# Sums of messages and of their squares: a TensorE product of the messages with themselves in place of a VectorE accumulator

## The reference, cut to what matters

```
h    = relu(layernorm(x))
node = mlp(h, W_node);  edge = mlp(edge_attr, W_edge)
msg  = relu([h[src], h[dst], edge] @ W_msg + b_msg)        # 100000 x 96
mu   = mean(msg, axis=0);  var = mean((msg - mu)**2, axis=0)
msg  = gamma * (msg - mu) * rsqrt(var + eps) + beta
out  = x + segment_sum(msg, dst) + node
```

## Time and profile before

| | us |
|---|---|
| median of 3 runs | 1090.58 (1089.98 to 1091.89) |
| profiled execution, its own time | 1093.96 |
| its span, first to last instruction | 1092.2 |
| PE busy | 839.5 (77%) |
| DVE busy | 724.6 (66%) |
| ACT busy | 542.9 (50%) |
| POOL busy | 826.6 (76%) |

### The profile page before, as it was taken

One profiled execution on the slowest core, in us unless ns is written; L12 is line 12 of the kernel. 1 busy time (PEld: TensorE's weight loads), 2 busy tenths in 40 slices (PEclk: granted clock), 3 DMA queues, 4 the chain that ended last, 5 costly groups with the idle time before them and its releaser, 6 DMA issues.

```text
span 1092.2 us, 23979 instructions
## 1 busy us (share of the span) xinstructions
PE 839.5 (77%) x6383; PEld 726.1 (66%) x6385; DVE 724.6 (66%) x1579; ACT 542.9 (50%) x1012; POOL 826.6 (76%) x786
## 2 busy tenths in 40 slices
PE   2537866639999999999777777777777776877777
PEld 2425622229999999999666666667667666766663
DVE  8678799978898898988444454444444444444445
ACT  3735988836666666666333333333333333333330
POOL 6877777777777777777777777777777777777771
PEclk9867988869999999999888888887898887888889
DMA  8665333352222222222222222222222222222223
GB/s 278 184 225 135 75 85 89 86 150 60 61 57 65 60 58 63 61 59 62 54 49 53 51 52 50 55 49 50 49 56 49 51 54 50 53 49 53 51 45 96
DMA packets 79842, 82.82 MB, mean 76 GB/s; under 512 B 52322, under 2 KB 57074, under 8 KB 79690
## 3 DMA queue, kind: packets, MB, share of 16 engines
q0 software_dynamic: 25024, 38.49, 16.6%
q1 hardware_dynamic: 54148, 42.83, 14.0%
q10 hardware_dynamic: 646, 1.25, 0.4%
HBM read 65.84 MB, written 13.34 MB: 72 GB/s over the span
## 4 chain that ended last, share of the span: by engine, by line
PE 31%; POOL 28%; issue 16%; DMA 11%; DVE 6%; ACT 5%; ACTq 0%; SPq 0%; DVEq 0%; POOLq 0%
POOL ring L455 28%; DMA ring<-p_table,src_idx 8%; PE pc L759 8%; PE pc L761 8%; PE pd L772 6%; DVE edge_st L936 4%; ACT r_sb L567 3%; DMA big_a<-acc 3%; PE pc L666 2%; PE pb L743 2%; PE pa L737 2%; PE pa L691 1%; DVE ln_buf L857 1%; ACT ring L515 1%; DVE ring L878 1%
## 5 line engine op out<-in xcount | busy, mean ns | idle before, releaser
L455 POOL DMA_INDIRECT ring<-p_table,src_idx x734 | 772.9, 1053 | 223.8 <-issue 199.7
L759 PE MATMUL pc<-w3c,r_sb 128*128 128x96 f32 x1564 | 334.0, 298 | 6.3 <-issue 5.9
L761 PE MATMUL pc<-q_win,hot_n 128*128 128x96 f32 x1564 | 322.7, 290 | 0.0
L1008 DVE TENSOR_TENSOR pc<-pc,ring 128x384 f32<-128x384 f32 x196 | 110.8, 565 | 315.3 <-POOLq L482 286.4
L618 ACT ACTIVATE msg<-pc 128x384 f32<-128x384 f32 x196 | 96.4, 492 | 438.3 <-DVE pc L1008 435.5
L772 PE MATMUL pd<-hot,msg 128*97 128x96 f32 x1564 | 192.2, 271 | 136.7 <-ACT msg L618 133.8
L759 PEld LDWEIGHTS pc<-w3c,r_sb 128*128 128x128 f32 x1564 | 262.5, 211 | 13.3 <-issue 10.7
L772 PEld LDWEIGHTS pd<-hot,msg 128*97 128x97 f32 x1564 | 165.8, 181 | 153.7 <-ACT msg L618 111.1
L761 PEld LDWEIGHTS pc<-q_win,hot_n 128*128 128x128 f32 x1564 | 258.6, 208 | 0.0
L1015 DVE TENSOR_TENSOR acc<-acc,msg 128x772 f32<-128x772 f32 x196 | 186.1, 950 | 0.0
L936 DVE BATCH_NORM_STATS2 edge_st<-r_sb 96x512 f32 (+1 forms) x196 | 121.2, 674 | 17.3 <-ACT r_sb L567 15.9
(11 more groups left out here) (110 smaller groups left out, 545.7 us busy)
## 6 DMA issues: line engine op xcount, KB each, us to landing
xs<-x_stack SPq DMA_DIRECT2D x196, 60.0 KB, 1.8
ring<-p_table,src_idx POOLq DMA_INDIRECT x734
q_win<-q_table SPq DMA_DIRECT2D x196, 36.0 KB
x_stack<-ring SPq DMA_DIRECT2D x6, 980.0 KB
ring<-in_x_nodes SPq DMA_DIRECT2D x5, 480.0 KB, 9.8
big_a<-acc SPq DMA_DIRECT2D x1, 2400.0 KB, 12.9
p_table<-ring SPq DMA_DIRECT2D x12, 192.0 KB, 2.5
q_table<-ring SPq DMA_DIRECT2D x12, 192.0 KB
```

Of the source, the lines that this page charges most:

```text
L455: nc.gpsimd.indirect_dma_start(out=ring[:, tile * C:(tile + 1) * C], out_offset=None, in_=table, in_offset=bass.IndirectOffsetOnAxis(ap=id ...
L759: nc.tensor.matmul(out, r_sb[:, j % 2, t * TILE:(t + 1) * TILE], w3c[:, :], start=True, stop=False)
L761: last = nc.tensor.matmul(out, hot_n[:, j % 2, t * TILE:(t + 1) * TILE], q_win[:, j, :], start=False, stop=True)
L1008: V.tensor_tensor(pc[:, j % 2, 0:n], pc[:, j % 2, 0:n], ring[:, bass.ds((g % RING) * (TPG * C), n)], ALU.add).then_inc(pre_added, 1)
```

## The change

The squares and the accumulator `acc` go. `msg` shrinks to 97 columns for each tile. Four more products for each group, of the messages of a tile with themselves, give a 97x97 matrix in `pd`, beside the window sum: its diagonal holds the sums of squares, its last column the sums. DVE adds it to `gram` in SBUF (97x97). At the end DVE multiplies `gram` with the identity and reduces it, in place of PE's sum over partitions. The zeros that two DMAs spread over `big_a` come from a tile of their own, `zeros`. The wait for `messages_done` moves behind the diagonal matrix, since only the products with `agg` need it, and the 5 products of `keep_clock(W_SUMS)` are gone. The core of the diff (declarations of semaphores, the two DMAs' source and the `Else` branch left out):

```
-        msg = sb("msg", [P, 2, TPG, MW])
-        acc = sb("acc", [P, TPG, MW])
+        msg = sb("msg", [P, 2, TPG, M1])
+        zeros = sb("zeros", [P, NP // 10])
+        gram = sb("gram", [M1, M1])
+        diag = sb("diag", [C, C])
...
                     wait(act, win_summed, g - 1)
-                    wait(act, acc_added, g - 1)
                     act.wait_ge(pre_added, g + 1)
                     nc.scalar.activation(msg[:, j % 2, 0:n, 0:C], ...
                                          ACT.Relu).then_inc(msg_relu, 1)
-                    act.wait_ge(msg_relu, g + 1)
-                    nc.scalar.square(msg[:, j % 2, 0:n, M1:MW], msg[:, j % 2, 0:n, 0:C]).then_inc(msg_square, 1)
...
                     pe.wait_ge(msg_relu, g + 1)
                     wait(pe, win_added, g - 1)
+                    for t in range(n):
+                        nc.tensor.matmul(pd[0:M1, j % 2, WIN:WIN + M1], msg[:, j % 2, t, :], msg[:, j % 2, t, :],
+                                         start=(t == 0), stop=(t == n - 1))
                     pe.wait_ge(hot_built, g + 1)
                     for t in range(n):
-                        last = nc.tensor.matmul(pd[0:M1, j % 2, 0:WIN], msg[:, j % 2, t, 0:M1], hot[:, j, t, :],
+                        last = nc.tensor.matmul(pd[0:M1, j % 2, 0:WIN], msg[:, j % 2, t, :], hot[:, j, t, :],
                                                 start=(t == 0), stop=(t == n - 1))
                     last.then_inc(win_summed, 1)
...
                 passes(pe, fast)
-                keep_clock(W_SUMS)
...
-            pe.wait_ge(messages_done, 1)
-            for k, lo in ((0, 0), (1, M1)):
-                for t in range(TPG):
-                    last = nc.tensor.matmul(pd[0:C, 0, k:k + 1], acc[:, t, lo:lo + C], ones[:, :],
-                                            start=(t == 0), stop=(t == TPG - 1))
-            last.then_inc(sums_made, 1)
             keep_clock(W_SCALES)
...
             pe.wait_ge(diag_kept, 1)
+            pe.wait_ge(messages_done, 1)
...
-            V.memset(acc[:, :, :], 0.0).then_inc(zeroed, 1)
+            V.memset(zeros[:, :], 0.0).then_inc(zeroed, 1)
+            V.memset(gram[:, :], 0.0)
...
-            far = msg[:, :, :, :].rearrange("p a t w -> p (a t w)")[:, 0:NTILES]
+            far = r_sb[:, 0, 0:NTILES]
...
                 def add_sums(i, j, base):
                     g, n = num(i, j), tiles(i, j)
-                    dve.wait_ge(msg_square, g + 1)
-                    wait(dve, acc_added, g)
-                    V.tensor_tensor(acc[:, 0:n, :], acc[:, 0:n, :], msg[:, j % 2, 0:n, :],
-                                    ALU.add).then_inc(acc_added, 1)
...
                     dve.wait_ge(win_summed, g + 1)
+                    wait(dve, gram_added, g)
+                    V.tensor_tensor(gram[:, :], gram[:, :], pd[0:M1, j % 2, WIN:WIN + M1],
+                                    ALU.add).then_inc(gram_added, 1)
                     wait(dve, win_added, g)
                     V.tensor_tensor(agg[:, bass.ds(base, WIN)], agg[:, bass.ds(base, WIN)], pd[0:M1, j % 2, 0:WIN],
                                     ALU.add).then_inc(win_added, 1)
...
                 passes(dve, fast)
+                dve.wait_ge(gram_added, NG)
+                dve.wait_ge(win_added, NG)
+                dve.sem_inc(messages_done, 1)
...
-            dve.wait_ge(sums_made, 1)
-            link(V.tensor_scalar(sc[:, 0:2], pd[0:C, 0, 0:2], 1.0 / E, None, ALU.mult))
+            link(V.tensor_tensor(diag[:, :], gram[0:C, 0:C], ident[0:C, 0:C], ALU.mult))
+            link(V.tensor_reduce(sc[:, 1:2], diag[:, :], AX, ALU.add))
+            V.tensor_scalar(sc[:, 0:1], gram[0:C, C:M1], 1.0 / E, None, ALU.mult)
+            link(V.tensor_scalar(sc[:, 1:2], sc[:, 1:2], 1.0 / E, None, ALU.mult))
```

More of the change, by code:

```diff
@@ L210, in graph_layer @@
         msg_relu = sem("msg_relu")
-        msg_square = sem("msg_square")
         win_summed = sem("win_summed")
         win_added = sem("win_added")
-        acc_added = sem("acc_added")
+        gram_added = sem("gram_added")
         node_added = sem("node_added")
@@ L226, in graph_layer @@
         gen_msg = sem("gen_msg")
-        gen_square = sem("gen_square")
+        gen_gram = sem("gen_gram")
         gen_hot = sem("gen_hot")
@@ L361, in _ @@
             sp.dma_start(big_a[C:P, :].rearrange("c (a b) -> c a b", b=NP // 10),
-                         acc[0:P - C, :, :].rearrange("c t m -> c (t m)")[:, 0:NP // 10].unsqueeze(1).to_broadcast(
+                         zeros[0:P - C, :].unsqueeze(1).to_broadcast(
                              [P - C, 10, NP // 10])).then_inc(h_zeroed, 16)
@@ L399, in _ @@
             sp.dma_start(agg[0:C, :].rearrange("c (a b) -> c a b", b=NP // 10),
-                         acc[0:C, :, :].rearrange("c t m -> c (t m)")[:, 0:NP // 10].unsqueeze(1).to_broadcast(
+                         zeros[0:C, :].unsqueeze(1).to_broadcast(
                              [C, 10, NP // 10])).then_inc(agg_zeroed, 16)
             sp.dma_start(agg[C:M1, :].rearrange("c (a b) -> c a b", b=NP // 16),
-                         acc[C:M1, :, :].rearrange("c t m -> c (t m)")[:, 0:NP // 16].unsqueeze(1).to_broadcast(
+                         zeros[C:M1, 0:NP // 16].unsqueeze(1).to_broadcast(
                              [1, 16, NP // 16])).then_inc(agg_zeroed, 16)
@@ L800, in _ @@
                     last.then_inc(gen_sum, 1)
+                    pe.wait_ge(gen_msg, g + 1)
+                    for t in range(TPG):
+                        last = nc.tensor.matmul(pd[0:M1, 1, 0:M1], msg[:, 0, t, :], msg[:, 0, t, :],
+                                                start=(t == 0), stop=(t == TPG - 1))
+                    last.then_inc(gen_gram, 1)
                     with pe.Fori(0, GEN_WINS) as w:
-                        pe.wait_ge(gen_msg, g + 1)
                         pe.wait_ge(gen_hot, g * GEN_WINS + w + 1)
                         for t in range(TPG):
-                            last = nc.tensor.matmul(pd[0:M1, 0, 0:WIN], msg[:, 0, t, 0:M1], hot[:, 0, t, :],
+                            last = nc.tensor.matmul(pd[0:M1, 0, 0:WIN], msg[:, 0, t, :], hot[:, 0, t, :],
                                                     start=(t == 0), stop=(t == TPG - 1))
                         last.then_inc(gen_win, 1)
-            pe.wait_ge(messages_done, 1)
-            for k, lo in ((0, 0), (1, M1)):
-                for t in range(TPG):
-                    last = nc.tensor.matmul(pd[0:C, 0, k:k + 1], acc[:, t, lo:lo + C], ones[:, :],
-                                            start=(t == 0), stop=(t == TPG - 1))
-            last.then_inc(sums_made, 1)
             keep_clock(W_SCALES)
@@ L1054, in _ @@
                                     ALU.add).then_inc(gen_pre, 1)
-                    dve.wait_ge(gen_square, g + 1)
-                    V.tensor_tensor(acc[:, :, :], acc[:, :, :], msg[:, 0, :, :], ALU.add).then_inc(gen_step, 1)
+                    dve.wait_ge(gen_gram, g + 1)
+                    V.tensor_tensor(gram[:, :], gram[:, :], pd[0:M1, 1, 0:M1], ALU.add).then_inc(gen_step, 1)
                     with dve.Fori(0, GEN_WINS) as w:
```

4 lines of the change are left out of this document (removed).

## The result

The changed kernel takes 1032.0 us (median of 4 runs, 1028.8 to 1033.2), the one before 1090.8: a ratio of 0.946, 95% interval 0.943 to 0.948. The prediction was 1048, with a range of 1027 to 1078: 4% less was forecast and 5.4% less measured, at the lower edge of what the forecast's own mechanism was given (1032 to 1063). The profiled execution has a span of 1031.4 us.

The account below looks back on a forecast made before the run. POOL's gather pitch bounds the kernel: 245 us, plus 496 (first stage) and 285 (second), puts the last gather at 1026; adding 24.2 less 0.7 gives a 1049.5 us span, 1048 on the median's scale, range 1027 to 1078.

Parts of the forecast that it names:

- What bounds the kernel: Loop over the groups: POOL's gather pitch sets the end; PE's speed only sets where the first stage ends.
- What the change removes: DVE loses L1015, 0.95 us in each of 196 groups, the longest of three operations that hold a gather back.
- PE's group: First stage: four new products add 0.70 us to PE's 2.94, giving 3.64 us for a group.
- The slower rival: PE bounds the whole loop: gain gone at 4.23 us a group, some 1114 us at half-clock prices; chance 0.06.
- The first stage's pitch: L994 and L997 hold gathers at a random phase by 0.08 us on average: pitch 1.33 us, before 1.46.
- The check of the formula against the kernel before: Random-phase sum for the first stage before the change: 1.25 + 0.26 against a measured 1.46, called somewhat pessimistic.
- The first stage's end: PE uses up the gathers' lead at t = 741 us, not 513, after 373 gathers at 1.33 us.
- The second stage's pitch: DVE in step with POOL, one-hots mostly miss the gathers' points: pitch 1.28 us, bounds 1.25 and 1.39.
- The tail: Behind the last gather: 24.2 us before the change, 0.7 us less after it.
- The fall of the clock: Output's 13 products: PE idle about 1 us ahead of the scale, up to 11 us lost; none taken.
- The rival built on it: POOL holds DVE: L994 and L997 each wait up to 0.82 us, DVE ends the loop, 1061 us; chance 0.03.
- the rival by which the stalls come back through them: Stalls move to L994 and L997: 1073 us with pitches 1.36 and 1.34, 1092 with 1.39 throughout; chance 0.15.

Follow-up runs that it names:

- the products twice: Changed kernel with the four products of the messages with themselves issued twice in each group: 1111.6 us, ratio 1.0183.
- the run with the bn_stats: Changed kernel with two one-input bn_stats over 128x386 of a scratch buffer where L1015 stood, result unread: 1045.4 us, ratio 0.9575.
- the run with 18 products: Changed kernel with 18 products that only keep the clock behind the loop (W_SCALES) in place of 9: 1029.5 us, ratio 0.9425.
- the add put back: Changed kernel with a 128x772 add from SBUF to a scratch buffer where L1015 stood, result unread: 1107.5 us, ratio 1.0145.
- before, add by tile: Kernel before with L1015 issued as four adds of 128x193 in place of one of 128x772: 1100.2 us, ratio 1.0078.
- before, no add: Kernel before without L1015, ACT's squares kept and no new PE products: 1039.3 us, ratio 0.9518.
- changed, one-hot by ACT: Changed kernel with 18 clock-keeping products and the float32 one-hot (L992) copied by ACT from the bf16 one: 1019.1 us, ratio 0.9332.
- changed, comparison with a scalar: Changed kernel with 18 clock-keeping products, float32 one-hot by ACT, and L989 made by four 128x96 comparisons with a per-partition scalar: 1013.5 us, ratio 0.9274.
- the one-hots by tile: Changed kernel with L989 and L992 issued as eight operations of 128x96 in place of two of 128x384: 1029.1 us, ratio 0.9417.

## Why the prediction was right, and where it was off

- **What bounds the kernel.** Right. The gathers' pitch set the end in every kernel but the one with the products twice, and in that one PE did.
- **What the change removes.** The mechanism was right: the add held the gathers. The run with it put back, the run with the same time in one-input operations, and the kernel before without it show it from three sides. The traces show it by a count as well, given below.
- **PE's group**, 3.64 us predicted, 3.63 measured, and hidden. The slower rival's sum held to some 5 us: worked out for 4.31 us a group, which is what the products twice make it (45 pieces each: 831 us x 45/8674), it gives 1106, and the time was 1111.6. Its 4.23 us is where the gain would be gone, not where PE begins to cost, which is about 3.9 by the estimate above.
- **The first stage's pitch** was the term of the sum that was mis-sized: 1.33 predicted, 1.28 measured. The last gather started 22 us earlier than forecast; at the 373 gathers that the forecast had at this pitch, 0.053 us each (567/444 is 1.277) is 20 us of it. Two things were wrong in it. I took an operation's whole 0.55 us as the stretch in which a gather can be caught. An operation must have begun ahead of the gather's start and end over 0.13 us behind it: with the 0.03 us of the rows above, that leaves 0.55 - 0.16 = 0.39 us. 2 x 0.39²/(2 x 3.63) = 0.04 gives 1.29, some 15 of the 20 us. The rest is that the phase is not random: PE's group and the gather fall into a pattern of 17 gathers in six groups, at 1.28. That this pattern is what makes 1.28 of 1.29 is read from the trace and was not tried. The check of the formula against the kernel before (1.51 for a measured 1.46) had shown a surplus, and I let it stand.
- **The first stage's end**, 741 predicted, 817 measured, follows from the pitch. **The second stage's pitch**, 1.28 predicted and 1.26 measured, was off by 2 us in 148 gathers. That the one-hots' place decides there was right: the run with the bn_stats moved them by 1 us and the pitch went to 1.36.
- **The tail**: 23.5 us from the last gather's start predicted, 27.1 measured. The fall of the clock behind the 9 products was named and priced at up to 11 us, and I took none. It cost 3.4 us by the run with 18 products. The reason I gave for none, longer idle times at a mean clock of 0.86, was a poor one: that mean is made of stretches at 0.50 as well.
- **The trace against the skill's rule.** The prediction said that POOL does not hold DVE. It does, for 0.06 us (L989's 0.62 for 0.56 above), not for the gather's whole 0.94. So the Trainium skill's page on SBUF (SBUF — State Buffer, the section on the two separate sides) is right that either side can be the one that waits; its "for the whole instruction" is not what these rows show for an indirect gather. The rival built on it, 1061 us, did not come.
- 22 us less up to the last gather, by the two pitches, and 3.6 us more in the tail make up the span's 18 us (1049.5 forecast, 1031.4 measured). That the time lies within the range is no luck: the bound, the wait and the hiding were as forecast. The two errors of size had opposite signs, and the smaller one hid some of the larger.
- One price of a rival was misadded: 1.39 us throughout gives a last gather at 245 + 596 x 1.39 = 1073 and a time of some 1095, not 1092. It changes nothing.

The count by the traces: add up, from 245 us on, what each gather took over 0.944 us:

| kernel | sum of the excess, us | last gather starts, us | difference |
|---|---|---|---|
| before | 79.6 | 1068.0 | 988.4 |
| changed | 16.5 | 1004.3 | 987.8 |
| the add put back | 93.3 | 1080.8 | 987.5 |
| two bn_stats | 31.1 | 1017.9 | 986.8 |
| before, add by tile | 88.2 | 1075.6 | 987.4 |
| before, no add | 25.3 | 1013.4 | 988.1 |
| changed, one-hot by ACT | 6.6 | 994.8 | 988.2 |
| changed, comparison with a scalar | 1.4 | 988.6 | 987.2 |

The difference is the same to 3 us in all eleven kernels with a trace, those not listed too (986.8 to 989.6): what moves the last gather's start is the excess and nothing else. And of the 1873 gathers with an excess over 0.012 us, 1856 have one that is the time from the gather's start to the end of a DVE operation of the kind named here, less 0.127 us, to 0.012 us. L1015 had 70.3 us of before's 79.6 and the one-hots 9.4; in the changed kernel the one-hots have 16.1. So the rival by which the stalls come back through them was there too, with 7 us.

What stays open: when a gather waits for one operation and when for two in a row. In the earlier trace rows and in the changed kernel's first stage it got through between L994 and L997 (there L989 and L992), where the second had begun behind it; in the run with the bn_stats, in the kernel before with its add by tile and in some groups of the one-hots by tile it was held on to the end of the next one. The traces sort the pairs of one-hots in part. Where DVE had stood idle for over 0.06 us just ahead of the first, the gather passed between the two in 415 of 416 cases, over seven kernels; where it hadn't, the gather was held to the second's end in 87 of 94, and six of the seven others stand at the start of the loop, where one pair follows another. That is a pattern in the traces, not a cause: no run changes the idle time alone.

## What to carry to other kernels

Where GpSimd's indirect gathers set the pace, look in the timeline at what DVE runs when a gather takes longer than its shortest: moving an operation with two SBUF inputs to a PSUM input, to ACT or to TensorE can be worth more than its busy time suggests: 0.95 us in each of 196 groups held gathers for 70 us, and with it went 59 us of the time. Cutting it into pieces issued back to back gained next to nothing in one kernel here (1029.1 for 1032.0) and lost 8 us in the other, and there that was not for the pieces' own holds but for the work that they pushed back. So look also at what stands behind the operation that you move or cut. PE work is a good place for it as long as PE's time for all groups stays below the gathers' time; work out that threshold first, since past it PE sets the end. When work between the last products and the next ones is removed or moved, recount the products that keep the clock.

## What the runs showed of the hardware that I had not expected

- A gather can hold DVE too, but shortly: L989 took 0.62 us for 0.56 when it began 0.03 us ahead of the gather, and 0.56 when it began 0.03 us after it. How far ahead an operation must begin to hold the gather is not the same for all: `add_node`'s, begun 0.07 to 0.09 us ahead in the run with the one-hots by tile, itself took 0.05 to 0.06 us longer, and the gather did not.
- Two operations with two SBUF inputs issued back to back can hold a gather together: 1.60 us and 1.70 us for 0.94, with no single operation over 0.55 us under way. Often they don't: a gather that began in a series of four adds passed after the one under way (600.11 above).
- A comparison with a scalar for each partition, one streamed input in SBUF, 128x96, holds a gather too, but four of them in each group cost 1.2 us in the whole kernel: pitch 1.25.
- Operations with at most one input in SBUF were otherwise harmless: of 428 gathers that began in the middle of an add with one input in PSUM and of no other, over all the traces, three had an excess, under 0.02 us each, and of 139 that began in the middle of a bn_stats none.
